# Attention operands moved by two heads instead of four, and products of the identity at the seams between passes

## The reference

```python
x = layernorm(x + attn(x))         # gated feed-forward, I = 2752
x = layernorm(x + xattn(x, ctx))   # cross-attention, 32 heads, 8 key heads, head size 32
x = layernorm(x + ffn(x))          # one linear layer, int4 weights, bf16
# attn:  s = silu(x @ w_gate.T); the half of each row with the smallest |s| is set to 0;
#        (s * (x @ w_up.T)) @ w_down.T
# xattn: softmax(q @ k.T * 32 ** -0.5) @ v @ Wo, each key head shared by 4 query heads
# ffn:   y = x.bf16 @ ((w_int - zeros) * scales).bf16.T
```

## Time and profile before

| | us |
|---|---|
| three runs | 2545.92, 2547.3, 2553.11 (median 2547.3) |
| the profiled execution | 2557.08 |
| its span | 2555.3 |
| PE busy | 2423.3 (95%) |
| DVE, ACT, POOL busy | 1264.0 (49%), 1045.8 (41%), 1414.6 (55%) |

### The profile page before, as it was taken

How to read it: one execution, slowest core, us unless ns; L and a number is a source line. 1 busy time by engine, 2 the same in 40 slices (tenths; PEclk the granted TensorE clock), 3 DMA queues, 4 the chain that set the end, 5 groups by cost and what they waited for, 6 DMA issues and landing times. The chain is left out here.

```text
span 2555.3 us, 32587 instructions
## 1 busy us (share of the span) xinstructions
PE 2423.3 (95%) x12640; PEld 2106.2 (82%) x12640; DVE 1264.0 (49%) x1775; ACT 1045.8 (41%) x1531; POOL 1414.6 (55%) x630
## 2 busy tenths in 40 slices
PE   7999899999999999999999999999988888888998
PEld 6999899988999889999889998899966565565775
DVE  3772303961017830069400485345467776664665
ACT  2112234533337333364323553233267676672211
POOL 5343244865447755458554585454378787783221
PEclk9999899999999999999999999999989898898999
DMA  5555522333333333233333233689957675556773
GB/s 195 175 194 169 205 94 92 107 120 126 117 101 103 122 118 119 99 100 123 111 118 116 96 108 100 192 252 291 256 159 176 161 170 142 140 139 164 178 174 98
DMA packets 245995, 371.70 MB, mean 145 GB/s; under 512 B 124336, under 2 KB 176560, under 8 KB 245584
## 3 DMA queue, kind: packets, MB, share of 16 engines
q1 hardware_dynamic: 245840, 369.60, 48.7%
HBM read 290.15 MB, written 78.70 MB: 144 GB/s over the span
## 5 line engine op out<-in xcount | busy, mean ns | idle before, releaser
L968 POOL TENSOR_TENSOR gp_w_lo<-cy_raw,gp_w_hi 128x1024 fp32r<-128x1024 f32 (+2 forms) x300 | 724.5, 2416 | 614.2 <-ACT gp_w_hi L847 613.7
L180 PE MATMUL gp_acc<-gp_x_hi,gp_w_hi 128*128 128x448 f32 x1504 | 561.0, 373 | 11.1 <-DVE gp_x_lo L1065 8.6
L181 PE MATMUL gp_acc<-gp_x_lo,gp_w_hi 128*128 128x448 f32 x1504 | 552.1, 367 | 0.0
L182 PE MATMUL gp_acc<-gp_x_hi,gp_w_lo 128*128 128x448 f32 x1504 | 551.9, 367 | 0.0
L847 ACT CAST gp_w_hi<-cy_raw 128x1024 fp32r<-128x1024 f32 (+2 forms) x300 | 307.1, 1026 | 308.6 <-PE gp_acc L182 307.1
L1413 POOL TENSOR_TENSOR ap_e_lo<-ap_e,ap_e_hi 125x1344 fp32r<-125x1344 f32 x112 | 341.7, 3072 | 99.4 <-DVE ap_e_hi L1494 69.0
L180 PEld LDWEIGHTS gp_acc<-gp_x_hi,gp_w_hi 128*128 128x128 f32 x1504 | 284.2, 189 | 35.8 <-issue 7.4
L182 PEld LDWEIGHTS gp_acc<-gp_x_hi,gp_w_lo 128*128 128x128 f32 x1504 | 284.2, 189 | 22.4
L181 PEld LDWEIGHTS gp_acc<-gp_x_lo,gp_w_hi 128*128 128x128 f32 x1504 | 284.6, 189 | 21.0
L464 DVE TENSOR_REDUCE gp_sel_unit<-gp_keys 112x4 f32<-112x2048 f32 x4 | 9.1, 2286 | 549.5 <-ACT gp_keys L860 549.5
L180 PE MATMUL gp_acc<-gp_h_hi,gp_w_hi 128*128 128x448 f32 (+1 forms) x704 | 267.3, 380 | 8.4 <-DVE gp_h_lo L1030 5.6
(11 more groups left out here) (192 smaller groups left out, 4350.4 us busy)
## 6 DMA issues: line engine op xcount, KB each, us to landing
cy_raw<-in_w_gu SPq DMA_DIRECT2D x172, 512.0 KB, 3.2
cy_raw<-in_w_d SPq DMA_DIRECT2D x80, 512.0 KB, 3.5
cp_c_raw<-in_ctx_t SPq DMA_DIRECT2D x32, 750.0 KB, 6.5
cy_raw<-in_w_q SPq DMA_DIRECT2D x32, 512.0 KB, 4.1
q_scratch<-gp_q_out SPq DMA_DIRECT2D x64, 224.0 KB, 6.6
cy_qs<-q_scratch SPq DMA_DIRECT2D x32, 448.0 KB, 5.4
k_scratch<-cp_k_out SPq DMA_DIRECT2D x16, 752.0 KB
cy_ks<-k_scratch SPq DMA_DIRECT2D x32, 376.0 KB, 7.0
```

The source lines that it names most:

```text
L180: nc.tensor.matmul(out, wh, xh, start=first, stop=False)
L181: nc.tensor.matmul(out, wh, xl, start=False, stop=False)
L182: return nc.tensor.matmul(out, wl, xh, start=False, stop=last)
L968: last = nc.gpsimd.tensor_tensor(o, i, hi.bitcast(F32), ALU.subtract)
```

## The change

Four edits.

**1. Quarters.** Queries, keys, maxima and both scratch tensors are laid out in quarters of two heads (`NQK` = 4). `fetch_qk` brings a quarter with four DMAs of half the row length, and its order in `attend_pass` is another: quarter 0, 1 and 2 of batch n + 2 at heads 2, 4 and 6 of batch n, quarter 3 at head 0 of batch n + 1. The values' fetch moves from head 3 to 5, the load of Wo from 2 to 3. `put_recip` and DVE's reciprocal move to score 22. `k_scratch` is stored with two DMAs a batch.

**2. Products of the identity with itself** (`keep_busy`, fp32, 128 x 128 or 128 x 112, into a bank that is overwritten later): 66 at the start and 10 at the end of `context_pass`, 14 and 9 in `gated_query_pass`, 10 at the start of `attend_pass`, 8 at the start of `finish_pass`.

**3. The start of `gated_query_pass`.** All four quarters of x are loaded during `context_pass`, the last two in the slots of weight tiles 2 and 3, which are loaded once `gp_x_lo` has read them. ACT splits tile 0, then x, then tiles 1 and 2; `gp_w_lo` of tile 0 is on DVE.

**4. The last batch.** Low parts of heads 2, 5 and 7 are on DVE (`LO_LAST`), and the quotients stand behind scores 14 and 17 instead of 17 and 20.

```diff
+NQK = 4
-        self.qs[0] = m.sb("qs0", [3 * HD + 2, 2, REP, 4, S], F32R)
+        self.qs[0] = m.sb("qs0", [3 * HD + 2, NQK, REP, 2, S], F32R)
...
+        key = kd[n, 2 * (f % 2) + f // 2]
+        for dst, src in ((q_rows[0:2 * HD], qd[n, f]), (k_rows[0:HD], key[0:HD]),
+                         (q_rows[2 * HD:stack], qd[n, f, 0:HD]), (k_rows[HD:stack], key)):
+            sp.dma_start(dst, src).then_inc(self.qk_loaded[p][f], 16)
...
+def keep_busy(nc, bank, ident_f, times):
+
+    rows = bank.shape[0]
+    for _ in range(times):
+        nc.tensor.matmul(bank, ident_f[:, 0:rows], ident_f[:], start=True, stop=True)
...
+    FIRST, LAST = 66, 10
...
+            pe.wait_ge(evac, NB * (B - 1) + 1)
+            keep_busy(nc, pk[0][:, 0:P], ident_f, LAST)
...
+            dve.wait_ge(hi_done, 1)
+            nc.vector.tensor_tensor(w_lo[0][:], raw[0][:], w_hi[0][:].bitcast(F32), ALU.subtract).then_inc(lo_done, 1)
...
-    RECIP_AT = 20
-    QUOTIENTS_AT = (17, 20)
+    RECIP_AT = 22
+    QUOTIENTS_AT = (14, 17)
...
-    W_LOAD_AT, W_SPLIT_AT = 2, 6
+    W_LOAD_AT, W_SPLIT_AT = 3, 6
+    V_AT = 5
+    FIRST = 10
+    LO_LAST = (2, 5, 7)
...
-            def fetch_qk(n, half):
+            def fetch_qk(n, f):
                 if n >= 2:
-                    sp.wait_ge(t_scored, NX * (n - 2) + NX // 2 * (half + 1))
+                    sp.wait_ge(t_scored, NX * (n - 2) + NX // NQK * (f + 1))
...
+            fetch_qk(1, NQK - 2)
+            cy.await_queries(sp)
...
+                    if h == 0 and n + 1 < B:
+                        fetch_qk(n + 1, NQK - 1)
+                    if h in (2, 4, 6) and n + 2 < B:
+                        fetch_qk(n + 2, h // 2 - 1)
...
-                if g % KV in LO_POOL:
+                if g % KV in LO_POOL and not by_dve(g):
```

More of the change, by code:

```diff
@@ L114, in __init__ @@
         self.q_stored = [m.sem(f"q_stored{i}") for i in range(self.NQO)]
[L115 removed]
+        self.qk_loaded = [[m.sem(f"qk_loaded{i}{f}") for f in range(NQK)] for i in range(2)]
         self.v_loaded = [m.sem(f"v_loaded{i}") for i in range(2)]
@@ L817, in _ @@
                         sp.wait_ge(s, 32 * KD // NQO)
-                    cy.fetch_qk(sp, q_v, k_v, 0, 0)
+                    for f in range(2):
+                        cy.fetch_qk(sp, q_v, k_v, 0, f)
                 if p == 23:
-                    cy.fetch_qk(sp, q_v, k_v, 0, 1)
+                    for f in range(2, NQK):
+                        cy.fetch_qk(sp, q_v, k_v, 0, f)
                 if p == 26:
@@ L826, in _ @@
                     sp.wait_ge(back, 2 * B)
-                    cy.fetch_qk(sp, q_v, k_v, 1, 0)
+                    for f in range(2):
+                        cy.fetch_qk(sp, q_v, k_v, 1, f)
                 if p == 32:
@@ L988, in _ @@
             pool.wait_ge(pads, 1)
-            for i in range(SPL):
-                split_lo(i)
+            pool.wait_ge(lo_done, 1)
+            for n in range(1, SPL):
+                split_lo(n)
             for g in range(G):
@@ L1330, in await_hi, with by_dve, lo_of_pool @@
                 eng.wait_ge(hi_dve, upto(HI_DVE, g))
+        def by_dve(g):
+            return g // KV == B - 1 and g % KV in LO_LAST
+        def lo_of_pool(g):
+            return upto(LO_POOL, g) - sum(by_dve(x) for x in range(g + 1))
         def await_lo(eng, g):
-            eng.wait_ge(lo_pool, upto(LO_POOL, g))
+            if by_dve(g):
+                eng.wait_ge(lo_dve, LO_LAST.index(g % KV) + 1)
+            else:
+                eng.wait_ge(lo_pool, lo_of_pool(g))
         @block.sync
         def _(sp):
-            def fetch_qk(n, half):
+            def fetch_qk(n, f):
                 if n >= 2:
-                    sp.wait_ge(t_scored, NX * (n - 2) + NX // 2 * (half + 1))
-                cy.fetch_qk(sp, qd, kd, n, half)
+                    sp.wait_ge(t_scored, NX * (n - 2) + NX // NQK * (f + 1))
+                cy.fetch_qk(sp, qd, kd, n, f)
             def fetch_v(n):
@@ L1507, in quotients, with split_lo @@
                 nc.vector.tensor_tensor(cy.num[i][:], cy.num[i][:], cy.rec[i][:], ALU.mult).then_inc(cy.normed, 1)
+            def split_lo(g):
+                await_hi(dve, g)
+                dve.wait_ge(pv, g - NLO + 1)
+                nc.vector.tensor_tensor(e_lo[g % NLO][:], e[g % NE][:], e_hi[g % NHI][:].bitcast(F32),
+                                        ALU.subtract).then_inc(lo_dve, 1)
             def follow(g):
@@ L1542, in first_pair @@
                 for i in range(2):
-                    last = nc.tensor.matmul(p_s[y % 2][:, i, 0:CP], qs[p][0:STACK, half, 2 * a + i, h % 4, :],
-                                            ks[p][0:STACK, half, h % 4, :], start=True, stop=True)
+                    last = nc.tensor.matmul(p_s[y % 2][:, i, 0:CP], qs[p][0:STACK, f, 2 * a + i, h % 2, :],
+                                            ks[p][0:STACK, f, h % 2, :], start=True, stop=True)
                 last.then_inc(scored, 1)
```

122 lines of the change are left out of this document (65 added, 57 removed).

## The result

The changed kernel takes 2576.4 us (2575.5 to 2577.1, four runs) against 2546.6 (2544.1 to 2553.1): ratio 1.0113, interval 1.0094 to 1.0132. The forecast was 2481, range 2456 to 2508, with a chance of 0.04 for slower. The profiled execution has a span of 2573.6 us.

A forecast was written before the change was run, and what follows sets the result against it. It took PE's waits and the slower clock behind them to bound the attention pass, with POOL next. Terms of -52.3, -2.2, -7.3, -4.5, -2, 0 and +1.7 gave -66.6 us, scaled to 2481 us, range 2456 to 2508.

The forecast's parts named there:

- The key waits: Attention pass, main term: all ten of PE's waits for keys, 30.7 us, go with the earlier fetches in quarters.
- POOL is next: Attention pass: POOL then binds, at 25.4 us a batch with weights; 23.7 us a batch behind batch 7.
- The maxima's rows: Attention pass, rows needed at score 24: fetching a quarter just ahead of them costs under 1 us a batch.
- late maxima: Rival, attention pass: rows land late behind the third quarter, 2 us a batch, 24 us back, 2505 us; chance 0.22.
- The first seam: Start of the second pass: kept clock and earlier parts bring its first tile out sooner, -7.3 us.
- The start: Start of the kernel: products of the identity bring PE's half-clock work to full clock, -2.2 us.
- The last seam: Start of the last pass: eight products of the identity ahead of it cost +1.7 us of lost work.
- The reciprocals: Three batches of the attention pass: moved two scores later, behind `nm_lo`, they leave 0.5 us three times, 1.5.
- Slower by the number of rows: Rival, attention pass: DMA queues pay by row, not byte, so a batch needs 30 us; 2561 us, chance 0.04.

The follow-up runs named there:

- e3: Changed kernel with the maxima's rows issued ahead of quarter 2 and the values fetched at head 3: 2496.2 us, ratio 0.9744 to the kernel before.
- e2: Changed kernel with only the values' fetch put back at head 3: 2525.9 us, ratio 0.9868 to the kernel before.
- g4: g1 with the reciprocal back at score 20, ahead of the maxima's low part in DVE's order: ratio 0.9763 to the kernel before.
- g1: Changed kernel with rows ahead of quarter 2, values at head 3, quotients at old places and no products of the identity: 2486.9 us, ratio 0.9737.
- e4: Changed kernel keeping the layout in quarters, but with all fetches at their old places: 2531.6 us, ratio 0.9890 to the kernel before.
- e1: Changed kernel with the maxima's rows issued ahead of quarter 2 instead of behind it: 2531.5 us, ratio 0.9902 to the kernel before.

## Why the prediction was wrong

- **The key waits, right.** No wait for `cy_ks` in the changed kernel.
- **POOL is next: right, but not reached.** It is the releaser in e3 (10.3 us in nine waits), with batches of 24.7 and 23 us. In the changed kernel it is not the bound at all.
- **The maxima's rows: the step that failed.** "I take under 1 us, inside the 0.7 above", between 0 and 3 us. It measured 5.9 us of wait a batch (88.4 in 15) and low clock behind it: the pass took 451.8 us against 368.7 in e3 up to the last batch's first score, 83 us in 15 batches, 5.5 each. Two errors stand in it. The chain of 4.7 us was read in batch 14, in which no queries or keys are fetched ahead of the rows (DMA share 0.42 in the earlier trace rows); the row with traffic, 5.5 us in the earlier trace rows, was the typical one (median 5.4), and with the 2.5 us from the transpose to the second issue it was over six scores' time already. And the small waits of the earlier trace rows were taken as proof that the rows are in time, while the key waits of 3 us held PE in the same place. The rival "late maxima", with a chance of 0.22, named the mechanism and priced it at 2 us a batch.
- **What the change adds there** was seen (quarter 2 right ahead) but not the values, which move from head 3 to 5. I wrote of them only as a fetch in SP's list, not as 773 KB in the engines 6 us ahead of the rows. e2 shows that they are more than half of the loss (1.0113 to 0.9868, of the way to e3's 0.9744).
- **The seams.** The start was right (-2.1). The first seam's -7.3 came as -4.5 at the tile: the forecast followed PE, and ACT's table load behind the split of tile 2 set the end. Up to the attention pass another 6.1 us were won that no term had; in the other traces with the new start that stretch takes 1535.0 to 1541.5 us, which holds the 1541.2 of before, so they can be chance. The last seam cost 4.1 instead of 1.7: 2.3 by the products, and 1.8 behind them, with the low stretch near the end.
- **The reciprocals**, priced at 16.4 - 1.5 us by their place: the wait for the denominators (6.75 us) is 0.7 in g4 at the old place, so it hung on the load of the engines; g4 is 8.6 us above g1, by rows that are late in the next batch.
- **Slower by the number of rows**: refuted by e4. It gave 2561, near the 2576 that came, by a mechanism that isn't there; the new fetches of 94 and 188 KB land after 3.5 and 4.2 us, where those of 188 and 376 KB took 5.5 and 7.0. That is more than half the time for half the bytes, as by the smaller rate that the Trainium skill (DMA: Bandwidth & Descriptors, Bandwidth) gives for small DMAs, but also beside another load; the kernel paid nothing for it that e4 shows.

## What to carry to other kernels

A wait that is taken away may have covered another on the same engine: subtract it and follow each chain that ends near it (here the rows, landing 1 us behind the end of the key wait) to the time at which it would be needed then. A small transfer on the critical path is as late as the bytes that all queues have put into the DMA engines ahead of it, so place the large ones several microseconds ahead (here the values 11 us ahead and not 6) or some 2 us behind it; another queue does not help. Look at the single increments of a late transfer's semaphore: if only some are late, a few engines hold it, and what loads these few is to be found. Products that keep the clock up pay only where PE itself is late afterwards.

## What the runs showed of the hardware

- A transfer of 14 KB lands after 2.1 us where no large one is near ahead of it (median of g1), and after a median of 7.5 us behind 773 KB issued 6 us and 618 KB issued right ahead, by SP's queue or by ACT's alike (7.5 and 7.2 us).
- The increments of one transfer's semaphore can come in two groups: with 773 KB 5 to 6 us ahead, 22 of the 32 increments of two rows are there at 2.0 us and the last at 5.4 (e1).
- With the values ahead, 618 KB issued right behind the rows delay them as well (45.8 us of waits against 29.7 with 2 us between).
- At the start of the last pass PE runs at half clock for 5.1 us with work (before) and for 6.0 with products of the identity ahead (changed kernel). In seven of 17 traces the granted clock is at half once more for 3.4 us, 14 us before the end, and these seven take some 1.7 us longer for the rest of the pass.
